# One core of Trainium2: two inverse tiles used in turn and reordered gated outputs in a two-layer kernel's first loop

## What is computed

```
qkvz = h @ W_qkvz;  ba = h @ W_ba
q, k, v = silu(causal conv of 4 taps over q, k, v)
beta = sigmoid(b);  alpha = exp(-exp(A_log) * softplus(a + dt_bias))
q = l2norm(q) * DK ** -0.5;  k = l2norm(k)       # x * rsqrt(sum(x * x) + 1e-6)
step: S = S * a_t;  v_new = (v_t - S.k_t) * b_t;  S = S + k_t (x) v_new;  o = S.q_t
og = o * silu(z);  og = og * rsqrt(mean(og * og) + 1e-6) * norm_weight
x = x + ga * (og @ W_out)
```

## Time and profile before

| | |
|---|---|
| median of 3 runs | 1217.29 us (1217.04 to 1225.51) |
| the profiled execution | 1213.53 us |
| its span in the profile | 1211.8 us |
| lead-in, up to the first merge | about 120 us |
| loop over the 16 heads | up to about 1012 us; GpSimd's `vsc` instruction, one a head, starts at 428.03 us and again at 483.86 us, 55.83 us a head |
| feed-forward and second layer | the rest |

### The profile page before, as it was taken

How to read it: one execution, slowest core, us unless ns; L and a number is a source line. 1 busy time by engine, 2 the same in 40 slices (tenths; PEclk the granted TensorE clock), 3 DMA queues, 4 the chain that set the end, 5 groups by cost and what they waited for, 6 DMA issues and landing times. The chain is left out here.

```text
span 1211.8 us, 29974 instructions
## 1 busy us (share of the span) xinstructions
PE 1089.0 (90%) x10488; PEld 948.9 (78%) x10488; DVE 957.2 (79%) x2560; ACT 808.4 (67%) x2225; POOL 733.3 (61%) x1186
## 2 busy tenths in 40 slices
PE   6684799999999999999999999999998888999985
PEld 6583688988888888889898888888887776776754
DVE  6888689898989899999989898989982435328754
ACT  6342576777777777877777777777775764219873
POOL 3274677777777776787778777777777512014111
PEclk9886999999999999999999999999998999999988
DMA  5221226323131313132222313131314130011000
GB/s 186 65 60 36 86 48 73 58 67 80 45 90 41 82 43 106 35 90 56 68 57 68 90 41 83 41 82 33 72 39 126 34 105 1 1 37 39 2 19 18
DMA packets 140869, 72.79 MB, mean 60 GB/s; under 512 B 114184, under 2 KB 130064, under 8 KB 138800
## 3 DMA queue, kind: packets, MB, share of 16 engines
q1 hardware_dynamic: 140720, 70.88, 23.0%
HBM read 57.06 MB, written 13.78 MB: 58 GB/s over the span
## 5 line engine op out<-in xcount | busy, mean ns | idle before, releaser
L1076 POOL TENSOR_TENSOR Tn<-Tn,tmp 64x31 f32<-64x31 f32 (+15 forms) x496 | 280.3, 565 | 38.9
L1073 POOL TENSOR_TENSOR tmp<-DT,Tn 64x31 f32<-64x31 f32 (+15 forms) x496 | 251.6, 507 | 49.4 <-DMA DT<-blk_in_scratch 15.3
L866 DVE SCALAR_TENSOR_TENSOR cv<-bank,cw,cv 128x255 f32<-128x255 f32 (+2 forms) x384 | 155.1, 472 | 52.4 <-ACT cv L665 52.3
L866 DVE SCALAR_TENSOR_TENSOR cqk<-bank,cw,cqk 128x255 f32<-128x255 f32 (+2 forms) x384 | 154.9, 471 | 26.7 <-ACT cqk L665 26.7
L1049 POOL TENSOR_TENSOR ro<-ss,mhalf 128x4 f32<-128x4 f32 x64 | 68.6, 1072 | 130.9 <-issue 76.4
L935 DVE SCALAR_TENSOR_TENSOR BP<-bank,cj,E 128x512 f32<-128x512 f32 (+1 forms) x256 | 144.6, 611 | 2.5 <-DVE cj L916 0.3
L476 PE MATMUL bank<-wo,OTs 128*128 128x256 f32 x512 | 136.2, 394 | 1.5 <-ACT OTs L758 1.5
L727 ACT ACTIVATE junk<-og 128x129 f32<-128x129 f32 x256 | 79.4, 310 | 53.2 <-issue 41.7
L476 PEld LDWEIGHTS bank<-wo,OTs 128*128 128x128 f32 x512 | 89.9, 193 | 13.0 <-ACT OTs L758 2.0
L735 ACT ACTIVATE ogn<-og,ro 128x128 f32<-128x128 f32 x256 | 81.9, 396 | 21.3 <-POOL ro L1049 20.4
L315 PE MATMUL bank<-hh,wqk_hi 128*128 128x256 f32 x256 | 79.0, 309 | 14.8 <-DVE wqk_lo L885 11.2
(11 more groups left out here) (211 smaller groups left out, 3249.2 us busy)
## 6 DMA issues: line engine op xcount, KB each, us to landing
rvz<-in_L_attn_W_qkvz SPq DMA_DIRECT2D x16, 512.0 KB, 3.6
x<-alpha_scratch SPq DMA_DIRECT2D x8, 1024.0 KB, 5.6
alb<-alpha_scratch SPq DMA_DIRECT2D x7, 1024.0 KB, 4.7
rqk<-in_L_attn_W_qkvz SPq DMA_DIRECT2D x16, 256.0 KB, 2.6
wo<-in_L_attn_W_out SPq DMA_DIRECT2D x16, 256.0 KB, 3.6
blk_in_scratch<-BP SPq DMA_DIRECT2D x256, 16.0 KB, 1.5
DT<-blk_in_scratch SPq DMA_DIRECT2D x16, 256.0 KB, 3.5
tinv_scratch<-Tn SPq DMA_DIRECT2D x32, 128.0 KB, 2.2
```

The costliest lines, as they stand in the source:

```text
L866: nc.vector.scalar_tensor_tensor(d, bk[:, t * T:(t + 1) * T - s], cw[p][:, first + t, TAPS - 1 - s:TAPS - s], d, ALU.mult, ALU.add).then_i ...
L1073: pool_step_done(nc.gpsimd.tensor_tensor(t, Dm[:, j, j + 1:BLK].unsqueeze(2).broadcast_to([SLOTS, r, c]), Tn[:, j, 0:c].unsqueeze(1).broad ...
L1076: pool_step_done(nc.gpsimd.tensor_tensor(Tn[:, j + 1:BLK, 0:c], Tn[:, j + 1:BLK, 0:c], t, ALU.subtract), kh * NTS + 2 * j + 4)
```

## The change

1. **Two inverse tiles in turn.** `Tn`, `tmp` and `DT` have 128 partitions; head `kh` uses the 64 partitions of its parity (`own`). The transposed copy overwrites the blocks in `DT`. `Tn` is cleared and gets its diagonal once at the start; later only a select that zeroes the part above the diagonal is done (no MEMSET), and it waits for the DMAs of the head before.
2. **Norms of the keys** by products with the column of ones, like those of q: two products more in `pe_gram1`, the square over q and k (512 columns, not 256), no diagonal reductions; VectorE puts all four norms away in one instruction and waits for the whole gram first.
3. **Beta in place**: `cj` reads `beta` with a stride, no copy.
4. **Step 0's gated output first**: VectorE's `dve_og` stands ahead of the weight splits, and one pair of scans less is ahead of it; the E1 pair of the next group stands ahead of `dve_acc`, the E2 pair behind `dve_r2`. The scans left over go to step 1 (three) and step 2 (three). ScalarE does step 1's first `Y` ahead of `act_ss` of step 0.
5. **Splits**: the low q,k part goes from VectorE to GpSimd (step 0, behind `vsc`); the v,z split goes one head earlier: the high part to step 1, ahead of that step's `act_ss`, the low part to the end of step 3.
6. `SPLIT` becomes ((0, 14), (14, 17), (17, 24), (24, 31)), and GpSimd waits for its own `ro` and `vsc`.

```diff
+            def own(tile, kh):
+                return tile[kh % 2 * SLOTS:(kh % 2 + 1) * SLOTS]
...
             def pe_gram1(kh, p, b):
...
-                for c in range(NC):
-                    last = nc.tensor.matmul(bG2[:, 256 + c:257 + c], sqq[:, c * P:(c + 1) * P], ones[:, 0:1], start=True, stop=True)
+                for q in range(2):
+                    for c in range(NC):
+                        last = nc.tensor.matmul(bG2[:, 256 + 2 * q + c:257 + 2 * q + c], sqq[:, 1 - q, c * P:(c + 1) * P],
+                                                ones[:, 0:1], start=True, stop=True)
...
-                nc.scalar.activation(sqq[:], sqk[b % 2][:, 1], ACT.Square).then_inc(sem("square_q"), 1)
+                nc.scalar.activation(sqq[:], sqk[b % 2][:], ACT.Square).then_inc(sem("square_qk"), 1)
...
             def act_step(kh, p, b):
...
-                if last and merges(last[2]):
-                    act_ss(*last)
...
-                    splits(kh, p, b, act_split_qk, act_split_vz)
+                    if kh + 3 < NKH:
+                        act_split_qk(kh + 3, 1 - p)
                 else:
                     act_y(kh, p, b, 0)
+                    if merges(last[2]):
+                        act_ss(*last)
...
                     if vz:
                         act_silu_v(*vz)
+                    if b == 1 and kh + 2 < NKH:
+                        act_split_vz(kh + 2, p)
                     act_ss(kh, p, b)
...
             def dve_scales(kh, p, b):
...
-                for c, bk in enumerate((bG1, bG2)):
...
-                    nc.vector.tensor_tensor_reduce(diag[:], bk[:, 0:P], ident, 1.0, 1e-6, ALU.mult, ALU.add,
-                                                   nrm[p][:, b, 2 + c:3 + c]).then_inc(sem("nrm_k"), 1)
...
+                nc.vector.tensor_scalar(nrm[p][:, b], bG2[:, 256:260], 1e-6, None, ALU.add).then_inc(sem("nrm"), 1)
...
-            SPLIT = ((0, 14), (14, 18), (18, 25), (25, BLK - 1))
+            SPLIT = ((0, 14), (14, 17), (17, 24), (24, BLK - 1))
+
+            def pool_split_qk(kh, p):
+                wait(nc.gpsimd, "wqk_high", kh + 1)
+                nc.gpsimd.tensor_tensor(wqk[p][1][:], rqk[:], wqk[p][0][:].bitcast(F32), ALU.subtract).then_inc(sem("wqk_split"), 1)
...
             def pool_inverse_start(kh):
-                wait(nc.gpsimd, "t_out0", kh * 32)
-                wait(nc.gpsimd, "t_turned", 2 * kh)
-                pool_step_done(nc.gpsimd.memset(Tn[:], 0.0), kh * NTS + 1)
...
+                T = own(Tn, kh)
+                wait(nc.gpsimd, "t_out0", (kh - 1) * 32)
+                wait(nc.gpsimd, "t_turned", 2 * (kh - 1))
+                pool_step_done(nc.gpsimd.affine_select(out=T, in_=T, compare_op=ALU.is_ge, fill=0.0, base=0,
+                                                       pattern=[[-1, BLK], [1, BLK]], channel_multiplier=0), t_rows(kh, 0))
```

More of the change, by code:

```diff
@@ L282, in build, with t_base, t_rows @@
             bZ, bOT, bU = bV, bVT, bO
-            NTS = 2 + 2 * (BLK - 1)
+            def t_base(kh):
+                return kh * 2 * (BLK - 1) + max(kh - 2, 0)
+            def t_rows(kh, rows):
+                return t_base(kh) + (1 if kh >= 2 else 0) + 2 * rows
             def at(kh, b, per, k=0):
@@ L323, in pe_gram0 @@
                 wait(nc.tensor, "bp", at(kh, b, 4))
[L324 to L325 removed]
+                nc.tensor.matmul(bG1[:], sqk[i][:, 0, 0:P], sqk[i][:].rearrange("p x t -> p (x t)"), start=True, stop=True)
             def pe_gram1(kh, p, b):
@@ L747, in act_turn @@
             def act_turn(kh, half):
-                wait(nc.scalar, "t_step", kh * NTS + (2 + BLK - 2 if half == 0 else NTS))
-                wait(nc.scalar, "t_out1", kh * 32)
+                wait(nc.scalar, "t_step", t_rows(kh, BLK // 2 - 1 if half == 0 else BLK - 1))
+                wait(nc.scalar, "t_out1", (kh - 1) * 32)
                 rows = slice(half * BLK // 2, (half + 1) * BLK // 2)
-                nc.scalar.activation(Tt[:, :, rows], Tn[:, rows, :].rearrange("s j i -> s i j"), ACT.Copy).then_inc(sem("t_turned"), 1)
+                nc.scalar.activation(own(DT, kh)[:, :, rows], own(Tn, kh)[:, rows, :].rearrange("s j i -> s i j"), ACT.Copy).then_inc(sem("t_turned"), 1)
             def act_ots(kh, p, b):
@@ L975, in scans_ahead @@
                         scans(ahead[n], lo, hi)
-                if gram and gram[2] == 0:
-                    dve_bet(gram[0], gram[1])
                 if gram:
@@ L983, in dve_step @@
                     dve_bp(*gram, 0)
-                    dve_nrm_q(*gram)
                     dve_bp(*gram, 1)
@@ L999, in dve_step @@
                 if merges(b):
-                    scans_ahead(1)
                     dve_r2(kh, p, b)
-                    scans_ahead(2)
-                    splits(kh, p, b, dve_split_qk, dve_split_vz)
+                    scans_ahead(1, R)
+                    scans_ahead(2, 0, R)
                     dve_og(kh, p, b)
+                if b == B - 1 and kh + 2 < NKH:
+                    dve_split_vz(kh + 2, p)
             def dve_dequant(i, m):
@@ L1084, in pool_step @@
                 pool_ro(kh, p, b)
+                wait(nc.gpsimd, "ro", at(kh, b, 1, 1))
                 if b == 0 and kh + 1 < NKH:
                     pool_vpow(kh + 1, 1 - p)
+                    wait(nc.gpsimd, "vpow", kh + 2)
+                if b == 0 and kh + 3 < NKH:
+                    pool_split_qk(kh + 3, 1 - p)
+                    wait(nc.gpsimd, "wqk_split", kh + 4)
             def sp_load_qk(kh):
```

84 lines of the change are left out of this document (33 added, 51 removed).

## The result

The changed kernel takes 1236.59 us (median of 4 runs, 1234.73 to 1239.02) against 1217.16 us (4 runs, 1213.55 to 1225.51) for the kernel before, run beside it: a ratio of 1.0167, 95% interval 1.0137 to 1.0197. That is slower by over 1%, a case that the forecast gave 0.20, and outside the range by 1.6 us. The profiled execution took 1239.02 us with a span of 1237.3, 25.5 more than before's; the medians differ by less, 19.4, as the profiled execution of the kernel before was its fastest and that of the changed one its slowest.

What follows compares the result with a forecast made beforehand. TensorE, busy for 90% of the span, was taken as the bound. Terms 24.6 - 25.5 - 6.8 + 13 - 3 = +2.3 us on the profiled 1213.5, plus 3.8 to the median's scale, gave 1219.5 us, range 1204 to 1235.

Steps and rivals of the forecast that it cites:

- `Y` ahead of the sums: Step 1: TensorE's wait for Y goes, a wait of 1.0 us for ogn comes; -1.7 us a head.
- `R2`: Step 0: with one scan pair fewer ahead, TensorE's stall shrinks to the hand-over; -0.45 us a head.
- the last columns: Step 3: the inverse ends late for ScalarE's second copy, so TensorE's next gram stalls; +1.0 us a head.
- lead-in: Ahead of the loop, VectorE and ScalarE set the pace and cheaper grams save time; -3 us, bounds -4 to 0.
- Products: Four grams a head, each with two more norm products on TensorE at 0.44 us a gram; 1.76 us a head.
- VectorE loses about 3.5 us: VectorE's work per head shrinks by norms, beta copy and q,k split; costed at nothing, as TensorE's order covers it.
- fifteenth head -2.15: Step 0 and step 1 gains were counted over 15 heads, the grams over 14; -2.15 us for the fifteenth.
- A: Rival: the inverse is in time, so step 3's 1.0 us stall is absent; 1206.5 us, chance 0.26.
- B: Rival: GpSimd becomes the bound, its columns stretched by scans, ending the inverse over 1.5 us late; 1232.5 us, chance 0.16.
- C: Rival: something else delays step 1's Y, its 1.7 us wait remains while products are paid; 1245 us, chance 0.03.
- the split on GpSimd: The low q,k split takes 1.57 us on GpSimd, covered by one column step fewer and earlier ro; costed at nothing.

Runs made afterwards that it cites:

- b_ones: The kernel before with the keys' norms by products with ones alone, all orders as before: 1225.2 us, ratio 1.0037.
- a_cols: The changed kernel with the inverse's columns split over the steps as before (14, 4, 7, 6): 1221.6 us, ratio 1.0019.
- a_diag_cols: The changed kernel with the keys' norms from the diagonals and the inverse's columns split as before: 1203.55 us, ratio 0.9881.
- b_y_og: The kernel before with only step 1's first Y ahead of the sums and the gated output ahead of the weight splits: 1224.87 us, ratio 1.0041.
- b_y_vz: b_y_og with the v,z splits also taken out of the merge step, the q,k split staying on VectorE: 1202.7 us, ratio 0.984.
- a_qk: The changed kernel with the low q,k split on VectorE again, behind the gated output: 1240.34 us, ratio 1.0169.
- a_scan: The changed kernel with the third scan of step 2 put back into step 1: 1225.88 us, ratio 1.006.
- a_diag: The changed kernel with the keys' norms from the diagonals again, by two VectorE reductions: 1223.91 us, ratio 1.0032.
- a_best2: The changed kernel with diagonal norms, columns as before, third scan back in step 1, second inverse copy behind q,k silu: 1196.12 us, ratio 0.9809.

## Why the prediction was wrong

The waits went and came where the forecast put them, but the sum was 0.86 us a head too low: +0.61 forecast (1.76 - 1.7 - 0.45 + 1.0), +1.47 measured. Over 14 heads that is 12 of the 17 us between the forecast and the median. The step that failed is the size of four terms of the sum, all off to one side: `Y` ahead of the sums at -1.7 us a head (measured -1.37), `R2` at -0.45 (-0.29), the last columns at +1.0 (+1.19), and the third scan's delay of step 2's gram, put at nothing without a word (+0.20). Outside these heads the lead-in's -3 us was not there. One mechanism was wrong as well, though it did not move the sum: the relief of VectorE, below.

- *Products, +1.76 us a head: right in sum.* Steps 2, 3 and 0 of b_ones show 0.44 to 0.55 a gram, a_cols against a_diag_cols 1.71 a head in all. That the total agrees so well is in part luck: by step it is 0.02 to 0.74, as other chains hide or stretch it.
- *"VectorE loses about 3.5 us ... I cost this at nothing there: TensorE's order covers it": wrong in its reason, not in its number.* b_ones shows the relief by the products to be worth 1.28 us in step 1, where TensorE waits for what VectorE releases. The gain that I gave to the order alone needs that relief or that of the splits: in b_y_og the order has none and loses, in b_y_vz it has the split's 1.2 us and gets 1.29. In the changed kernel both reliefs are there, and there the relief by the products shows no gain beside the other (a_cols against a_diag_cols, step 1: the products cost 0.63 us and give nothing back). So nothing was the right number beside -1.7, but VectorE's share of busy time was no ground for it: VectorE was in the chain to the stall.
- *Y ahead of the sums, -1.7: mis-sized, -1.37.* The wait of 1.0 us for `ogn` was as forecast. Of the missing 0.33 us, 0.19 is `ro` itself, 1.20 us instead of 1.01 (last section); in a_qk, where it takes 1.01, step 1 is 0.18 shorter, and where the products are taken out and it takes 1.01 again, step 1 falls by 0.63, which is 0.44 and 0.19 (so this 0.19 is also in the 1.71 above). The other 0.14 stays open.
- *R2 in step 0, -0.45: mis-sized, -0.29.* VectorE now waits 0.56 us for solve 1, as forecast, but its subtraction and the hand-over stay between two products of TensorE:

```profile
486.72 0.42 DVE L930 TENSOR_TENSOR R<-Vs,bank 128x256 f32<-128x256 f32 x1 [0.56 <-PE bank L451]
...
487.20 0.30 PEld L451 LDWEIGHTS bank<-R,UT 128*128 128x128 f32 x2 [0.32 <-DVE R L930]
```

- *Last columns, +1.0: right in place, +1.19.* Sums later by the third scan, the column behind `ro`: a_scan and a_cols each remove their part, 0.5 and 1.1 us of step 3. The same scan also makes step 2's gram late, +0.20 net of the products (a_scan takes 0.34 off that step), and this I had not priced: I followed the scan to the sums and not to the q,k silu, which follows the same taps.
- *Lead-in -3, fifteenth head -2.15: not there in the profiled execution,* where the first `ro` comes 2.1 us later and the forecast had the loop start 3 us earlier. Over the profiles of all runs a lead-in gain can be seen at the first `vsc` and is lost in the scatter by the first `ro`. The first `vsc` starts at 59.8 us on average in the six profiles with reductions and at 57.2 in the eight with products; the first `ro` at 148.5 and 146.9, but with a spread from 144.0 to 152.6. b_y_og has the lead-in code of the kernel before, and its first `ro` comes at 151.03, before's at 146.05. The row of 50 to 70 us tells them apart, first before's, then b_y_og's:

```profile
50.00:70.00 20.00, 15.78 (x108) 13.85 (x108) 15.62 (x46) 5.02 (x11) 5.22 (x9) 0.83 0.28 81
```

```profile
50.00:70.00 20.00, 16.18 (x69) 14.98 (x69) 12.93 (x39) 3.37 (x8) 5.25 (x8) 0.50 0.30 79
```

  Same instructions, a granted clock of 0.83 in the one and 0.50 (all of it at the 1.2 GHz level) in the other, and 108 matmuls done against 69. In the two last heads it is alike: 83.03 us at 0.94 in the changed kernel, 78.79 at 1.00 in a_cols, whose code there differs in nothing but columns of an inverse.

```profile
954.20:1037.23 83.03, 67.37 (x624) 59.30 (x622) 33.00 (x81) 52.09 (x156) 30.50 (x47) 0.94 0.18 56
```

```profile
939.46:1018.25 78.79, 63.33 (x624) 55.43 (x622) 32.91 (x81) 51.91 (x156) 30.70 (x46) 1.00 0.21 58
```

  Some 4 us either way in the lead-in and again in the tail come and go with that clock, which may be why the 31 runs of the kernel before in one group spread from 1210.18 to 1226.98 us: the four fastest of them have a mean granted clock of 0.965 to 0.969, the five slowest 0.956 to 0.958. What raises or lowers it in one execution and not in the next stays open.

Of the rivals, A fell (the inverse is late), C fell (no `Y` wait), and B came half way: GpSimd's chain does set step 3, as the 1.77 us of a_diag show, but ScalarE waits 1.25 to 1.34 us, not the 1.5 from which B was to decide, and the split on GpSimd, which was to be part of it, costs nothing. Nor did scans stretch GpSimd's columns: by the pages its products take 251.3 us in all (251.6 before) and its subtractions 275.5 (280.3 before). What made the difference was no rival but the terms above, all off to one side, and a range that took each rival alone and not these together.

## What to carry to other kernels

Where a stall ends a chain that another engine feeds, the relief of that engine and the reordering of what hangs on it are not two gains to be added (here 1.28 us by relief alone, 1.29 by order and relief of another kind), so price them together: find what the moved work now stands ahead of (here the splits ahead of `R`). An instruction that is moved delays everything behind it on its engine, not only the consumer one looks at; list each of the next three and price them all. And a term that rests on a part of the program at changing clock should enter the range, not the sum.

## What was not expected of the hardware

GpSimd's `ro` of step 0, 128x4 and always the same work, takes 1.20 us or 1.01, by 0.1 us in the start of a scan on VectorE. In the changed kernel the first of a pair of scans starts at 494.07, 0.02 us ahead of the `ro` at 494.09 above, which takes 1.20:

```profile
494.07 0.41 DVE L892 TENSOR_TENSOR_SCAN E<-alb,eye 128x128 f32<-128x128 f32 x1
```

In a_qk the `ro` starts first, by 0.08 us, and takes 1.01, though the same scans run beside it:

```profile
498.78 1.01 POOL L1043 TENSOR_TENSOR ro<-ss,mhalf 128x4 f32<-128x4 f32 x1 [4.45 <-issue]
```

```profile
498.86 0.73 DVE L892 TENSOR_TENSOR_SCAN E<-alb,eye 128x128 f32<-128x128 f32 x2
```

So it is not what runs beside it that tells, but which of the two started first. The Trainium skill ("SBUF — State Buffer", section "Who interferes with whom") says so: the two engines share a pair of ports, a VectorE instruction with two inputs in SBUF contends there with a GpSimd one that reads SBUF, and the order of issue, not the shape, decides which engine blocks. In the order the rows agree. The size fits a full wait too, though `ro` loses only 0.19 us where the scan has 0.39 to go: `ro` ends at 495.29, 0.80 us behind the scan's end at 494.48. In a_best2 a longer scan has 0.65 us to go, and `ro` again ends 0.80 us behind it:

```profile
451.36 0.69 DVE L891 TENSOR_TENSOR_SCAN E<-alb,eye 128x256 f32<-128x256 f32 x1
```

```profile
451.40 1.45 POOL L1054 TENSOR_TENSOR ro<-ss,mhalf 128x4 f32<-128x4 f32 x1 [3.22 <-issue]
```

In the first fourteen heads of all 14 profiles there are 223 such `ro`, started while a VectorE instruction with two inputs in SBUF had over 0.25 us to go and no other began within 0.1: 217 of them end 0.80 to 0.82 us behind its end, and the other six, all of b_y_vz, 0.88. With 0.2 us or less to go nothing is lost. It is as if the first 0.2 us of `ro`'s 1.01 did not need what the scan holds; why, no run shows. The median over 12 heads of the changed kernel is 1.19, so 0.02 us of order repeats from head to head, and with `ro` in the chain to the turn it is paid each time.
